# A two-layer adaLN model on one core: routing from logits, token slots and scales as rows by DMA, statistics inside the feed-forward, a new order between the layers, part of k*v on GpSimd

## The reference, cut to what matters

```python
# layer 0, first part: a recurrence over time, 16 heads of 8 x 8 state
def step(S, inps):
    rt, kt, vt, dt = inps
    kv = kt[..., :, None] * vt[..., None, :]
    o = jnp.einsum('bhk,bhkv->bhv', rt, S + u[None, :, :, None] * kv)
    S = dt[..., None] * S + kv
# group norm, gate, projection Wo, rms norm, and a gelu feed-forward 128 -> 512 -> 128
# layer 0, second part: one of 8 experts for each token, at most 128 tokens for an expert
logits = x @ w_switch + b_switch
probs = jax.nn.softmax(logits, axis=-1)
pmax = probs.max(axis=-1)
routes = probs.argmax(axis=-1)
pos = (jnp.cumsum(oh, axis=0) * oh).sum(-1) - 1
keep = pos < capacity
slot = jnp.where(keep, routes * capacity + pos, E * capacity)
out = jnp.where(keep[:, None], y_flat[slot], x)
scale = pmax / jax.lax.stop_gradient(pmax)
# layer 1, first part (a selective scan, 256 channels, 16 states each)
xz = x @ in_proj;  u = silu(causal conv of the first half);  zb = second half
state = decay * state + dt_t[..., None] * b_t[:, None, :] * u_t[..., None]
y = (sum over states of state * c + D * u) * silu(zb)
# layer 1, second part: 16 gated experts, 8 for each token, and a shared one
```

## Time and profile before

| | |
|---|---|
| time, median of 3 runs | 735.65 us (728.85 to 738.16) |
| the profiled execution | 734.84 us, its span 733.0 us |
| busy share of the span | PE 81%, DVE 79%, POOL 53%, ACT 52% |
| chain that ended last | PE 44%, DVE 19%, POOL 15%, issue 12%, ACT 7% |
| mean granted clock of PE | 0.903 |

### The profile page before, as it was taken

One profiled execution on the slowest core, in us unless ns is written; L12 is line 12 of the kernel. 1 busy time (PEld: TensorE's weight loads), 2 busy tenths in 40 slices (PEclk: granted clock), 3 DMA queues, 4 the chain that ended last, 5 costly groups with the idle time before them and its releaser, 6 DMA issues.

```text
span 733.0 us, 6710 instructions
## 1 busy us (share of the span) xinstructions
PE 594.7 (81%) x1900; PEld 330.7 (45%) x1900; DVE 575.9 (79%) x751; ACT 380.2 (52%) x657; POOL 388.8 (53%) x330
## 2 busy tenths in 40 slices
PE   6596776579789996888866878678776997999997
PEld 3232232147557752323322333223233775778885
DVE  0866996736576668339999999999998894888886
ACT  4474000687454246567655565465555445465553
POOL 0005666344000020127899989887777564577775
PEclk9698656779889999869999999999999998999999
DMA  8000001600000000100000001000100422334440
GB/s 298 3 2 0 0 1 29 277 0 1 0 1 1 1 0 0 43 1 0 0 0 23 21 22 44 21 11 2 44 0 12 145 98 78 103 117 136 119 120 14
DMA packets 13380, 32.84 MB, mean 45 GB/s; under 512 B 1792, under 2 KB 2048, under 8 KB 12864
## 3 DMA queue, kind: packets, MB, share of 16 engines
q1 hardware_dynamic: 13344, 32.42, 13.6%
HBM read 31.24 MB, written 1.18 MB: 44 GB/s over the span
## 4 chain that ended last, share of the span: by engine, by line
PE 44%; DVE 19%; POOL 15%; issue 12%; ACT 7%; DMA 1%; POOLq 0%; DVEq 0%; SPq 0%; ACTq 0%
PE ps L895 16%; POOL arena L1641 13%; DVE arena L1559 7%; PE ps L578 5%; DVE arena L1536 4%; PE ps L846 3%; PE ps L793 2%; PE ps L706 2%; PE ps L744 2%; POOL h_parts L1746 2%; PE ps L761 1%; DVE arena L1350 1%; PE ps L729 1%; PE ps L806 1%; PE ps L646 1%
## 5 line engine op out<-in xcount | busy, mean ns | idle before, releaser
L1641 POOL TENSOR_TENSOR arena<-arena 128x512 f32<-128x512 f32 x186 | 229.8, 1261 | 72.1 <-DVE arena L1559 34.1
L1559 DVE TENSOR_TENSOR_SCAN arena<-ps,carry,arena 128x512 f32<-128x512 f32 x128 | 156.4, 1262 | 0.0
L1207 ACT ACTIVATE ps<-arena,abase 128x512 f32<-128x512 f32 x128 | 88.1, 691 | 91.3 <-DVE arena L1559 91.2
L846 PE MATMUL ps<-arena,core 128*128 128x512 f32 x256 | 130.8, 635 | 0.0
L1746 POOL TENSOR_TENSOR h_parts<-arena,h_parts 128x512 fp32r<-128x512 f32 x68 | 99.2, 1473 | 58.2 <-ACT h_parts L1240 55.5
L895 PE MATMUL ps<-x_parts,w_hi 128*128 128x512 f32 x272 | 100.8, 410 | 3.0 <-DVE arena L1559 2.5
L931 PE MATMUL ps<-bc,sel 96*128 96x512 bf16 x128 | 45.0, 412 | 56.2 <-DVE arena L1536 41.0
L1536 DVE TENSOR_TENSOR arena<-ps,arena 128x1024 f32<-128x1024 f32 x64 | 76.8, 1200 | 6.7 <-PE ps L931 6.6
L1634 DVE TENSOR_TENSOR arena<-arena 128x512 f32<-128x512 f32 x64 | 73.0, 1140 | 2.2
L846 PEld LDWEIGHTS ps<-arena,core 128*128 128x128 f32 x256 | 52.6, 206 | 40.9 <-issue 31.9
L1629 DVE TENSOR_TENSOR arena<-ps,arena 128x512 f32<-128x512 f32 x68 | 46.4, 683 | 27.2 <-PE ps L895 19.6
(11 more groups left out here) (216 smaller groups left out, 973.3 us busy)
## 6 DMA issues: line engine op xcount, KB each, us to landing
arena<-weight_rows SPq DMA_DIRECT2D x64, 256.0 KB, 3.3
arena<-in_wB SPq DMA_DIRECT2D x2, 2048.0 KB, 12.6
arena<-in_wD SPq DMA_DIRECT2D x8, 384.0 KB, 3.1
arena<-in_cstB SPq DMA_DIRECT2D x1, 1368.0 KB, 5.9
x<-in_x SPq DMA_DIRECT2D x4, 256.0 KB, 4.8
out_x<-x SPq DMA_DIRECT2D x4, 256.0 KB, 2.1
arena<-in_wA SPq DMA_DIRECT2D x1, 928.0 KB, 9.7
wC<-in_wC SPq DMA_DIRECT2D x1, 912.0 KB, 11.2
```

The lines of the kernel that those rows point to most:

```text
L846: mm(bank(c + 2 * (i % 2)), CORE_("eye"), PRC[:, (2 * q + c) % PR_RING, :], start=(n == 0), stop=(n == NS - 1)).then_inc(*done(f"y{n}_{c}" ...
L1207: A(bank(6 + c), ch(DTG[:, c, :], i), ACT.Exp, scale=ABASE[:, c * NS + n:c * NS + n + 1]).then_inc(*done(f"dec{n}_{c}", i))
L1559: nc.vector.tensor_tensor_scan(ST[:, k % ST_RING, :], bank(6 + c), DBU[:, (2 * q + c) % DBU_RING, :], CARRY[:, k:k + 1], ALU.mult, ALU.add ...
L1641: mul = lambda o, a, b: nc.gpsimd.tensor_tensor(o, a, b, ALU.mult)
```

## The change

- Recurrence: `kv_aside` picks 2 of the 8 turns of a chunk, 8 of 32. For these ACT copies the spread row out of PSUM (`spread_copy`) and POOL multiplies it by k; the scan of such a turn reads k*v from SBUF and the decay from a PSUM bank, to which ACT copies it once for each chunk (`decay_bank`).
- Feed-forward: `centreD` and `sqD` of chunks 0 and 1 move into the feed-forward, the ends of the two others are interleaved with the first `lnD`, and DVE adds the residual ahead of its second `f_lo`.
- Router: the expert is taken from the logits and not from the probabilities; the steps ahead of `r_oh` go from 10 to 5 and those after it from 12 to 8, and six steps of the scale move in between the one-hot matrices of the dispatch. `totals` is written in the order that the scan reads.
- Slots and scales: a PE transpose of a 128x16 tile, one ACT copy, one DMA to DRAM and four broadcast loads each (`slot_row`, `scale_row`), in place of 32 ACT diagonals, 8 PE matmuls of 512 columns and 8 ACT copies.
- Experts: the bias is added by DVE (`y_sum`), from which `y_hi` and `y_lo` are made; `e_relu` runs on DVE for 3 and 6 (and 0), on ACT else; `kept_x` moves behind the loop.
- Between the layers: `xb(3)` goes ahead of `z(0)`; `z` of chunks 1 to 3 moves into the scan's turns 10 to 15, as tanh, a half, an add of one (ACT) and a product (POOL) in place of silu; `bc` no longer waits for `z_silu` but for `u1`; the gates of the scan move by one turn, and `dtg` and `du` by up to 5.

The diff, cut to its core:

```diff
-GATE_PE = {0: [("gate0", 1)], 1: [("gate1", 1)], 2: [("gate0", 2)], 3: [("gate1", 2)],
-           4: [("gate0a", 3)], 5: [("gate0", 3)], 6: [("gate1a", 3)], 7: [("gate1", 3)]}
-GATE_ACT = {1: (0, 1), 2: (1, 1), 3: (0, 2), 4: (1, 2), 6: (0, 3), 8: (1, 3)}
...
+GATE_PE = {1: [("gate0", 1)], 2: [("gate1", 1)], 3: [("gate0", 2)], 4: [("gate1a", 2)], 5: [("gate1", 2)],
+           6: [("gate0a", 3)], 7: [("gate0", 3)], 8: [("gate1a", 3)], 9: [("gate1", 3)],
+           10: [("z0", 2)], 11: [("z1", 2)], 12: [("z0", 3)], 13: [("z1", 3)], 14: [("z0", 1)], 15: [("z1", 1)]}
+GATE_ACT = {2: ("gate", 0, 1), 3: ("gate", 1, 1), 4: ("gate", 0, 2), 6: ("gate", 1, 2), 8: ("gate", 0, 3), 10: ("gate", 1, 3),
+            11: ("z", 0, 2), 12: ("z", 1, 2), 13: ("z", 0, 3), 14: ("z", 1, 3), 15: ("z", 0, 1), 16: ("z", 1, 1)}
+STEP_POOL = {4: ("dtg_0", 1), 6: ("dtg_1", 1), 8: ("du_0", 1), 10: ("du_1", 1), 12: ("z0_full", 2), 14: ("z1_full", 2), 15: ("z0_full", 3), 16: ("z1_full", 3),
+             17: ("dtg_0", 2), 20: ("dtg_1", 2), 21: ("du_0", 2), 24: ("du_1", 2), 25: ("z0_full", 1), 28: ("z1_full", 1),
+             29: ("dtg_0", 3), 32: ("dtg_1", 3), 36: ("du_0", 3), 40: ("du_1", 3)}
 C_RING, DBU_RING, PR_RING, ST_RING = 4, 6, 2 * LAG, 8
 ROUTE_SCALE = 2.826
...
+KV_AHEAD = 4
+
+
+def kv_aside(q):
+
+    return q < NR and q % DK in (3, 7)
...
+    add(dve, ln_dve, one(*R_STEPS[:8]), [("h_turned_lo", 0)], one(*R_STEPS[8:]))
+    for t in range(NT):
+        if t % 4 == 2 and t < NT - 4:
+            dve.append(("h_turned_lo", t // 4 + 1))
+        dve.append(("onehot", t))
+        if t in SCALE_STEPS:
+            dve.append((SCALE_STEPS[t], 0))
...
-        pe += [("e_down", e)] + ([("e_up", e + 2)] if e + 2 < E0 else []) + ([("scale_spread", e)] if e < NCH else [])
-        act += [("y_hi", e)] + ([("e_relu", e + 2)] if e + 2 < E0 and e % 2 else []) + ([("scales", e)] if e < NCH else [])
-        dve += [(f"place{(3 * e + j) % E0}", (3 * e + j) // E0) for j in range(3)] + \
-            [("y_lo", e)] + ([("e_relu", e + 2)] if e + 2 < E0 and e % 2 == 0 else []) + ([("kept_x", e)] if e < NCH else [])
+        pe += [("e_down", e)] + ([("e_up", e + 2)] if e + 2 < E0 else [])
+        act += [("y_hi", e)] + ([("e_relu", e + 2)] if e + 2 < E0 and e + 2 not in RELU_DVE else [])
+        dve += [(f"place{(3 * e + j) % E0}", (3 * e + j) // E0) for j in range(2)] + [("y_sum", e), (f"place{(3 * e + 2) % E0}", (3 * e + 2) // E0)] + \
+            ([("e_relu", e + 2)] if e + 2 in RELU_DVE else []) + [("y_lo", e)]
...
-        [("centreE", 2), ("varE", 2)], xb(1), [("centreE", 3), ("varE", 3)], xb(2), z(0), xb(3),
-        [("bc", 0), ("gate0", 0)], z(1), [("gate1", 0), ("bc", 1)], dt(0), z(2), dt(1), [("bc", 2)], z(3), dt(2), [("bc", 3)], dt(3))
+        [("centreE", 2), ("varE", 2)], xb(1), [("centreE", 3), ("varE", 3)], xb(2), xb(3), z(0),
+        [("bc", 0), ("gate0", 0), ("bc", 1), ("gate1", 0), ("bc", 2)], dt(0), [("bc", 3)], dt(1), dt(2), dt(3))
...
-        xb_copy(2), u(0), xb_copy(3), z_silu(0), raw(0), [("gate0_tanh", 0)], u(1), [("bc_mid", 0)], z_silu(1), [("gate1_tanh", 0)], raw(1),
-        u(2), z_silu(2), [("bc_mid", 1)], raw(2), u(3), z_silu(3), sp(0), [("bc_mid", 2)], raw(3), sp(1), sp(2), sp(3), [("bc_mid", 3)])
...
+        xb_copy(2), u(0), xb_copy(3), z_silu(0), raw(0), u(1), [("gate0_tanh", 0)], raw(1), u(2), [("gate1_tanh", 0)], raw(2), u(3),
+        [("bc_mid", 0)], sp(0), raw(3), [("bc_mid", 1)], sp(1), [("bc_mid", 2), ("bc_mid", 3)], sp(2), sp(3))
+    add(dve, [("kept_x", 0), ("kept_x", 1)], sums(0), places(3), one("xb_zero"), [("kept_x", 2)], sums(1), norm_e(0), [("kept_x", 3)], sums(2), norm_e(1), sums(3), conv(0, 0), norm_e(2), conv(1, 0), norm_e(3),
+        conv(0, 1), conv(1, 1), conv(0, 2), conv(1, 2), [("bc_r1", 0)], conv(0, 3), conv(1, 3), one("a_neg", "st_zero"), [("bc_r1", 1), ("bc_r1", 2), ("bc_r1", 3)],
...
+SCALE_AT = NT - 5
+RELU_DVE = (3, 6)
+R_STEPS = ["r_logit", "r_max", "r_hit", "r_rank", "r_best", "r_oh", "r_shift", "r_base", "r_cum", "r_pos", "r_own", "r_place", "r_slot", "r_kept"]
+SCALE_STEPS = {3: "r_sum", 4: "r_recip", 5: "r_prob", 6: "r_pmax", 7: "r_precip", 8: "r_scale"}
...
+            for k, (row, dst, landed) in enumerate((("slot_row", SLB, slots_loaded), ("scale_row", SCB, scales_loaded))):
+                sp.wait_ge(*upto(row))
+                sp.dma_start(token_rows[k].rearrange("c (t p) -> (c t) p", p=P), TOKEN_ROW[k]).then_inc(token_kept, 16)
+                sp.wait_ge(token_kept, 16 * (k + 1))
+                for i in range(NCH):
+                    sp.dma_start(ch(dst, i), token_rows[k][i:i + 1, :].partition_broadcast(P)).then_inc(landed[i], 16)
...
-                        pe.wait_ge(*column("scan{}", q - 4))
+                        pe.wait_ge(*column("spread_copy{}" if kv_aside(q - 4) else "scan{}", q - 4))
...
+            centre_d(2)
             var_d(0)
+            centre_d(3)
             var_d(1)
-            centre_d(NCH - 1)
...
             pe.wait_ge(*upto("r_oh"))
             mm(bank(1)[:, 0:P], CB_("tri"), small(3), start=True, stop=True).then_inc(*done("prefix"))
-            mm(bank(2)[:, 0:P], CB_("ones"), small(3), start=True, stop=True).then_inc(*done("totals"))
...
+            mm(bank(2)[:, 0:P].rearrange("p (e t) -> p e t", e=E0), CB_("ones"), small3(3).rearrange("p t e -> p e t"), start=True, stop=True).then_inc(*done("totals"))
+            for t in range(NT // 2, NT):
+                h_turn(t)
+            pe.wait_ge(*upto("r_kept"))
+            nc.tensor.transpose(bank(1, 0, NT)[:, 2 * P:3 * P], tiny(9), CORE_("eye")).then_inc(*done("slot_turn"))
...
+                if t == SCALE_AT:
+                    pe.wait_ge(*upto("r_scale"))
+                    nc.tensor.transpose(bank(2, 0, NT)[:, 2 * P:3 * P], tiny(4), CORE_("eye")).then_inc(*done("scale_turn"))
...
-                    pe.wait_ge(*upto("y_lo", e - 2))
+                    pe.wait_ge(*upto("y_sum", e - 2))
+                elif e == 0:
+                    pe.wait_ge(*upto("scale_row"))
                 o = bank(2 + e % 2)[:, 0:P]
-                a = cb_at["b2"][0] + e * P
-                mm(o, CB_("ones")[0:1, :], cstB[0:1, a:a + P], start=True, stop=False)
...
-                pe.wait_ge(*upto("z0_silu", i))
+                pe.wait_ge(*upto("u1", i))
+                if i == 0:
+                    pe.wait_ge(*upto("z0_silu", i))
...
+            for q in range(NR):
+                i, v = q // DK, ORDER[q % DK]
+                if q % DK == 0:
+                    if i >= 2:
+                        act.wait_ge(*upto(f"scan{ORDER[-1]}", i - 2))
+                    else:
+                        act.wait_ge(*upto("w_exp", NCH - 1))
+                    act.wait_ge(*upto("decay", i))
+                    A(bank(2 + i % 2), ch(DEC, i), ACT.Copy).then_inc(*done("decay_bank", i))
+                if kv_aside(q):
+                    act.wait_ge(*upto(f"spread{v}", i))
+                    if q >= 2 * KV_AHEAD:
+                        act.wait_ge(*column("scan{}", q - 2 * KV_AHEAD))
...
                 i, v = q // DK, ORDER[q % DK]
-                if q + 1 < NR:
+                if q + 1 < NR and not kv_aside(q + 1):
                     kv(q + 1)
+                if kv_aside(q):
+                    dve.wait_ge(*upto("decay_bank", i))
                 if q % DK == 0:
                     dve.wait_ge(*upto("decay", i))
                 dve.wait_ge(*upto(f"kv{v}", i))
-                nc.vector.tensor_tensor_scan(S[:, v, i * N + 1:(i + 1) * N + 1], ch(DEC, i), bank(4 + q % 4),
+                nc.vector.tensor_tensor_scan(S[:, v, i * N + 1:(i + 1) * N + 1], *((bank(2 + i % 2), KVX[:, (q // KV_AHEAD) % 2, :]) if kv_aside(q) else (ch(DEC, i), bank(4 + q % 4))),
                                              S[:, v, i * N:i * N + 1], ALU.mult, ALU.add).then_inc(*done(f"scan{v}", i))
...
+            def z_parts(c, i):
+                act.wait_ge(*upto(f"z{c}", i))
+                A(ZT[c, i], bank(2 + c), ACT.Tanh, scale=0.5).then_inc(*done(f"z{c}_tanh", i))
+                A(ch(Z[:, c, :], i), bank(2 + c), ACT.Copy, scale=0.5).then_inc(*done(f"z{c}_half", i))
+                act.wait_ge(*upto(f"z{c}_tanh", i))
+                A(ZT[c, i], ZT[c, i], ACT.Identity, bias=col("one")).then_inc(*done(f"z{c}_one", i))
...
+                    if j == 2:
+                        dve.wait_ge(*upto("e_down", e))
+                        if e >= 2:
+                            dve.wait_ge(*upto("y_lo", e - 2))
+                        tt(Y32[:, e % 2, :], bank(2 + e % 2)[:, 0:P], CB_("b2")[:, e * P:(e + 1) * P], ALU.add).then_inc(*done("y_sum", e))
...
+                tt(YB[:, 1, e, :], Y32[:, e % 2, :], YB[:, 0, e, :].bitcast(f32), ALU.subtract).then_inc(*done("y_lo", e))
...
+                stt(ch(HB, i), ch(HB, i), modcol(0, GB), ch(SCB, i), ALU.mult, ALU.mult).then_inc(*done("moe_scaled", i))
...
+            def kv_product(q):
+                i, v = q // DK, ORDER[q % DK]
```

(9 more changed lines are left out.)

319 lines of the change are left out of this document (169 added, 150 removed).

## The result

The changed kernel takes 713.88 us (median of 4 runs, 713.59 to 714.99), the one before 734.10 (median of 4, 728.85 to 738.16): a ratio of 0.973, 95% interval 0.969 to 0.978. The span of the profiled execution went from 733.0 to 711.8. The forecast was 702, range 692 to 713: 21 us came where 33 were expected.

A forecast was written before the change was run, and what follows sets the result against it. The prediction took the bound to change by stage: DVE in recurrence and layer 1's scan, PE in the last 170 us, step order between the layers. Terms summed to -33.1; 733.0 - 33.1 + 1.84 = 701.7, taken as 702, range 692 to 713.

The forecast's parts named there:

- Recurrence, -4.7: Recurrence: eight turns each lose 0.58 us as their k*v product goes from DVE to POOL, -4.7 us.
- the rival of two SBUF inputs: Recurrence: two SBUF inputs after all, or POOL full, costs 8 x 0.95, total 709.5 us; chance 0.08.
- it is done some 2.5 us after scan q: Recurrence: POOL's product kv(q+4), behind prod(q), is done some 2.5 us after scan q and wanted after 5.3.
- Feed-forward's end, -3.0: End of feed-forward up to r_logit: from 182.2, earlier centring and interleaved order bring r_logit to 192.6, -3.0 us (-2 to -3.5).
- Router's chain, -3.4: Router, r_logit to first dispatch: fewer steps make it 5.8 us where it was 9.2, -3.4 us (-2.5 to -3.6).
- Dispatch, -1.4: Dispatch: slot_spread goes, part of the low-clock cost may go, a transpose and scale steps come, -1.4 us (0 to -2.3).
- Experts, -4.0: Experts: PE loses bias and scale_spread, first e_up to last y_lo 19.8 us against 23.9, -4.0 us (-2 to -5.5).
- Combine, +0.4: Combine: kept_x(2) now stands before x_moe(1), on the path, +0.4 us (0 to +1).
- Between the layers, -18.0: Between the layers: reordered passes and silu moved out bring layer 1's first scan to 310.4 from 328.46, -18.0 us.
- PE's clock falls between the layers: Rival, between the layers: short gaps between PE's passes lower its clock, +6 us, total 708; chance 0.08.
- Scan of layer 1, +1.0: Scan of layer 1: extra POOL work in turns 12 to 36 causes small stalls, +1.0 us (0 to +7.4).
- the rival of a full GpSimd: Scan of layer 1: it becomes POOL's or ACT's, 702 + 6.4, total 708.5 us; chance 0.12.

The follow-up runs named there:

- run 2: Changed kernel with k*v one step later in GpSimd's queue, behind the read-out product of step q-3: 710.18 us, ratio 0.968.
- Run 1: Changed kernel with the feed-forward's centring product put back behind the down products: 705.74 us, ratio 0.962.
- run 9: Changed kernel with g_one of chunk 0 reading its input from PSUM in place of SBUF: 711.57 us, ratio 0.971.
- run 11: Changed kernel with three idle matmuls of 128x512 added on TensorE ahead of combine: 713.94 us, ratio 0.973.
- run 12: The best version with three idle matmuls added ahead of combine: 709.30 us, ratio 0.964.
- run 8: Changed kernel with centring product behind the down products, k*v one step later, and g_one as scalar_tensor_tensor: 703.81 us, ratio 0.959.
- run 10: The best version: changed kernel with centring product behind the down products, k*v one step later, g_one reading PSUM: 704.56 us, ratio 0.961.
- run 13: Changed kernel with centring product moved back, k*v one step later, and GpSimd waiting for g_one and g_sel: 705.31 us, ratio 0.960.
- run 14: The best version with chunk 0's g_sel reading PSUM too, and a small VectorE copy added: 702.92 us, ratio 0.962.
- run 6: Changed kernel without the six z products on GpSimd (computes something else, serves for the turns alone): 713.26 us, ratio 0.971.
- run 3: Changed kernel with the gating of chunk 0 begun at turn 43 of the scan in place of turn 34: 710.12 us, ratio 0.967.
- run 5: Changed kernel with g_one written as scalar_tensor_tensor, same result and place: 714.08 us, ratio 0.972.

## Why the prediction was wrong

The forecast was 11.9 us too good. By its own terms:

- **Recurrence, -4.7.** The scans gave -4.8; no scan suffers from its new operands, so the rival of two SBUF inputs is refuted. But the stage gave -3.2. The step that failed is "it is done some 2.5 us after scan q": ScalarE's copy isn't there that early, GpSimd waits 11.2 us for it, and at the end four products stand behind. I checked the queue's load and not its order. One step later in the queue brings 1.0 of the 1.6 back (run 2, and the five later kernels with it).
- **Feed-forward's end, -3.0.** The end itself gave -2.6. But I took it "from 182.2" as if the stretch ahead were unchanged, and it became 4 us longer. The centring product was moved forward of its input: x_attn isn't there when TensorE comes to it. Run 1 shows it whole: 4.1 us back by this product's place alone. And x_attn is late partly because it had been moved too: beside GpSimd's product it takes 1.36 us for 0.75, the price of two SBUF inputs that the prediction reads in the earlier trace rows and charges to the recurrence alone. A moved step was costed where it had stood and not where it went.
- **Router's chain, -3.4**: -3.15. **Dispatch, -1.4**: -2.4. **Experts, -4.0**: -5.4. All right in kind, the last two too small: the low clock of the dispatch went wholly (1.00 in this stretch). That is in part luck of the profile, since in runs 9, 11 and 12 the same dispatch took 1.4 to 1.6 us more. Why the experts gave more than forecast wasn't looked into.
- **Combine, +0.4**: +1.5, at a clock of 0.71; +0.0 in run 1 with the clock high. `kept_x` costs nothing.
- **Between the layers, -18.0**: -15.2, and -17.1 to -17.2 in runs 1, 8, 10, 13 and 14 at a higher clock. The mechanism was right. The rival "PE's clock falls between the layers" came in part, 1.9 us of its 6; more exactly, the clock was no lower than before (0.87 and 0.86 in the two windows), but the forecast had counted every pass at the full clock.
- **Scan of layer 1, +1.0**: +6.3. Rings and loads did hold: turns 10 to 27 are as long as before, and the rival of a full GpSimd is wrong in its mechanism, though the 7.4 us that it gives the stage were near. This is the term furthest off. The step that failed is the list of what could make this stage longer: rings, loads and small stalls, but no instruction of VectorE's. 4.8 us are one such instruction that GpSimd shut out; run 6 shows that the z products weren't needed for it, only that it now fell elsewhere among GpSimd's. I had weighed this contention for the recurrence alone, as a doubling of an instruction, and not asked which small instructions of the scan live in SBUF. Another 1.7 us are in turns 0 to 3; half or more of it is gone in run 1 and, with the same instructions there, in runs 2, 3 and 8 to 14.
- **The last stretch, no change**: -1.1, which no edit accounts for; over the runs it is 168.0 to 170.3.

The measured time lies 0.9 us above the range: a part of the clock rival's price came together with two losses that stood in no rival, the feed-forward's and the held instruction's, and with the queue's. The two rivals of +6.4 and +7.6 come to 708.4 and 709.6, 0.1 us beside what stands there, which changes nothing.

What runs 3, 5, 6, 9 and 13 show of the hold: it doesn't hang on `tensor_scalar` or `scalar_tensor_tensor`, nor on the z products; it needs the data in SBUF, and it ends within 0.1 us of GpSimd's last product before it stands still (runs 3, 5, 6 and 9) or is made to (`g_sel` in run 13; for `g_one` there it isn't shown). The Trainium skill ("SBUF — State Buffer", on its two sides) has VectorE and GpSimd share a port pair as an exclusive lock, taken by a VectorE instruction in a two-port mode or with two SBUF inputs, and held for one whole instruction. Which instructions were held agrees with that: `g_one` with one input in PSUM passed (0.20), the reciprocal with its one input passed (0.55), `g_sel` with two was held (3.63). For `g_one` as the change has it, with one input, it would have to be a two-port mode, and no run shows the mode. How long they were held does not agree: by a lock for one instruction `g_one` would have been let in 0.5 us later, at 428.94, and not after 4.9.

**What stays open**: why such an instruction is let in between two of GpSimd's at some times (`g_pick`, at 446.86 in the changed kernel with GpSimd at work, took no more than 0.34 us) and at others not, at four borders running; and what brings TensorE's clock down at `combine` and in the dt products. Filling one pause (runs 11 and 12) went with a clock of 1.00 at `combine` both times, but two profiles are few where runs without it show either clock; filling those between the layers wasn't tried.

## What to carry to other kernels

When a step moves to another place in a queue, ask first when its input is ready there, and what stands behind it; the load of the engine says nothing on that. Where GpSimd is packed and VectorE sets the time, look for small VectorE instructions that only touch SBUF: give them an operand in PSUM if the bank is free without a new wait, or let GpSimd wait for them once, which costs it nearly nothing when it has time to spare later. And compare stages from start to start, with the granted clock of each beside it, and not totals, where the start of the kernel wanders by 2 us and the clock's part by 8.

## What the runs showed of the hardware

- A VectorE add of 128x64 numbers in SBUF, 0.17 us when it gets in, stood 3.05 to 5.32 us beside unbroken GpSimd work (a reciprocal of the same size did not, 0.55 in all kernels). With one operand in PSUM it took 0.20 beside the same work.
- A VectorE instruction of 128x512 numbers with two inputs in SBUF took 0.75 us alone and 1.36 beside one GpSimd product.
- The same kernel at two speeds: the best version's times are 700.67 to 701.10 or 708.02 to 709.67, with the mean granted clock (0.923 to 0.928, or 0.913 to 0.915) going with them. The changed kernel's four times are all within 1.4 us.
